# Middle stage of a two-layer spectral convolution kernel: a new order of its product groups, last products in 512 columns, and three of sixteen split units on GpSimd

## The reference, cut to what matters

```python
# layer 0: group norm, upsample by 2, leaky ReLU, downsample by 2
x = x + _filtered_lrelu(_gn(x), f)
# layer 1: spectral convolution of the normalized result
def _contract_tt(xf, a, b, c, d):
    ac, bc, cc, dc = _c(a)[0], _c(b), _c(c), _c(d)[..., 0]
    o1 = jnp.einsum('jxk,ky,bcxy->jbcxy', cc, dc, xf)
    return jnp.einsum('oi,icj,jbcxy->boxy', ac, bc, o1)
x_ft = jnp.fft.rfft2(_gn(x))
out_ft[:, :, :64, :64]  = _contract_tt(x_ft[:, :, :64, :64],  a1, b1, c1, d1)
out_ft[:, :, -64:, :64] = _contract_tt(x_ft[:, :, -64:, :64], a2, b2, c2, d2)
x = x + jnp.fft.irfft2(out_ft, s=(128, 128))
```

## Time and profile before

| | |
|---|---|
| median of 3 runs | 5124.49 us (5120.15 to 5128.3) |
| the profiled execution | 5120.79 us, its span 5118.5 us |
| PE busy | 4679.6 us, 91% of the span |
| DVE busy | 3679.7 us, 72% |
| ACT busy | 3314.3 us, 65% |
| POOL busy | 2581.5 us, 50% |
| first unit to last out group (middle stage) | about 2773 to 4622 us |

### The profile page before, as it was taken

How to read it: one execution, slowest core, us unless ns; L and a number is a source line. 1 busy time by engine, 2 the same in 40 slices (tenths; PEclk the granted TensorE clock), 3 DMA queues, 4 the chain that set the end, 5 groups by cost and what they waited for, 6 DMA issues and landing times. The chain is left out here.

```text
span 5118.5 us, 246321 instructions
## 1 busy us (share of the span) xinstructions
PE 4679.6 (91%) x103206; PEld 4195.3 (82%) x103206; DVE 3679.7 (72%) x5675; ACT 3314.3 (65%) x5910; POOL 2581.5 (50%) x2950
## 2 busy tenths in 40 slices
PE   7999999999999999999984899898989898988999
PEld 6888888888888888888874888888888888888999
DVE  6676777777777777677767888888888888883333
ACT  6767767767677676776854666666666666662332
POOL 7767857768587586776841333333333333330000
PEclk9999999999999999999996999999999999999999
DMA  2131232232321313123232222222222222228999
GB/s 59 57 114 55 63 107 59 65 100 65 106 67 55 114 57 114 57 63 108 65 103 88 82 66 78 70 73 75 68 79 66 82 66 82 66 74 345 420 421 398
DMA packets 609976, 556.29 MB, mean 109 GB/s; under 512 B 16996, under 2 KB 543332, under 8 KB 592612
## 3 DMA queue, kind: packets, MB, share of 16 engines
q1 hardware_dynamic: 609380, 547.21, 32.1%
HBM read 278.71 MB, written 268.44 MB: 107 GB/s over the span
## 5 line engine op out<-in xcount | busy, mean ns | idle before, releaser
L1281 DVE TENSOR_TENSOR Ml<-ring,Mh 128x1024 f16<-128x1024 f32 x1024 | 1199.1, 1217 | 201.6 <-ACT Mh L1248 193.6
L1248 ACT ACTIVATE Mh<-ring 128x1024 f16<-128x1024 f32 x1024 | 986.5, 1022 | 301.5 <-PE ring L1182 301.1
L1182 PE MATMUL ring<-wcur,b_hi 64*128 64x128 f16 x16384 | 749.1, 217 | 176.5 <-DVE Ml L1281 137.2
L752 DVE SCALAR_TENSOR_TENSOR Y<-ring,Y 128x532 f16<-128x532 f32 x1024 | 682.0, 706 | 284.8 <-ACT Y L605 284.6
L267 POOL TENSOR_TENSOR A<-Af,A 128x788 f16<-128x788 f32 x512 | 862.8, 1685 | 41.4
L1182 PEld LDWEIGHTS ring<-wcur,b_hi 64*128 64x128 f16 x16384 | 610.6, 94 | 246.7 <-DVE Ml L1281 154.5
L605 ACT ACTIVATE Y<-ring 128x532 f16<-128x532 f32 x1024 | 575.1, 610 | 275.0 <-PE ring L367 262.2
L1182 PE MATMUL ring<-wcur,b_lo 64*128 64x128 f16 x8192 | 716.9, 217 | 0.0
L367 PE MATMUL ring<-uth,A 64*128 64x138 f16 x12288 | 605.7, 223 | 65.1 <-issue 31.4
L265 POOL CAST A<-Af 128x788 f16<-128x788 f32 x512 | 429.9, 840 | 279.1 <-ACT Af L583 275.2
L767 DVE TENSOR_TENSOR Z<-ring,Z 128x1024 f16<-128x1024 f32 x256 | 313.4, 1224 | 314.7 <-ACT Z L616 314.7
(11 more groups left out here) (153 smaller groups left out, 10436.1 us busy)
## 6 DMA issues: line engine op xcount, KB each, us to landing
xb<-in_x SPq DMA_DIRECT2D x258, 256.0 KB, 2.9
x<-x1b SPq DMA_DIRECT2D x64, 1024.0 KB, 6.4
spec<-sp_out SPq DMA_DIRECT2D x256, 256.0 KB, 3.5
xin<-spec SPq DMA_DIRECT2D x128, 512.0 KB, 6.4
fd<-ft SPq DMA_DIRECT2D x128, 512.0 KB, 4.1
F<-fd SPq DMA_DIRECT2D x64, 1024.0 KB, 20.1
xq<-x SPq DMA_DIRECT2D x64, 1024.0 KB, 16.9
out<-yq SPq DMA_DIRECT2D x64, 1024.0 KB, 18.5
```

The lines of the kernel that those rows point to most:

```text
L752: dve.scalar_tensor_tensor(out=Y[:, e, 1, m], in0=ring[:, pr[u], :, 0:UPS], scalar=0.0, in1=Y[:, e, 0, m], op0=ALU.max, op1=ALU.subtract). ...
L1182: mm = pe.matmul(ring[:, UNIT_PAIR[n], t, 128 * k:128 * k + 128], b[r, z, 4 * u + k, :], wcur[r, z, w, :], start=(part == 0), stop=(part = ...
L1248: act.activation(hi, ps, ACT.Copy).then_inc(e_hi, 1)
L1281: dve.tensor_tensor(lo, ps, hi, ALU.subtract).then_inc(e_lo, 1)
```

## The change

`GROUPS_AT` replaces the three tuples: two groups of app1 after unit 2 and two after unit 5, two out groups of the first spectrum ("out0") after unit 8, two groups of app0 after 11 and two after 13, two out groups of the second spectrum ("out1") after 15. An out group now takes one spectrum and the whole batch: two fp32 matmuls of 512 columns. ScalarE copies out0's result to a new tile `o0`, and VectorE combines `o0` with out1's PSUM result in four operations of 512 columns in place of eight of 256.

Units 1, 5 and 13 (`POOLED`) are no longer split from PSUM: ScalarE copies them in fp32 to a new tile `Mf` (two buffers), which releases the bank pair, and GpSimd makes high and low part from `Mf`. VectorE does nothing for them. GpSimd's list becomes `iteration`: two splits, the row copy of z = 0, the conversion of z = 1, the third split, the row copy of z = 1, the conversion of z = 0 for the next s. SyncE loads before it stores. The shared counters give way to one semaphore for each kind.

```diff
-APP1_AT, OUT_AT, APP0_AT = (3, 3, 5, 5), (7, 7, 9, 9), (11, 11, 14, 14)
+GROUPS_AT = (("app1", (2, 5)), ("out0", (8,)), ("app0", (11, 13)), ("out1", (15,)))
+POOLED = (1, 5, 13)
+DIRECT = tuple(n for n in range(16) if n not in POOLED)
...
+        def released(eng, s, n):
+            if n in POOLED:
+                wait(eng, e_cp, len(POOLED) * s + POOLED.index(n) + 1)
+            else:
+                wait(eng, e_lo, len(DIRECT) * s + DIRECT.index(n) + 1)
...  GpSimd
+            def split(s, i):
+                n = len(POOLED) * s + i + 1
+                _ps, hi, lo = unit(*divmod(POOLED[i], 8))
+                pool.wait_ge(e_cp, n)
+                carry(pool, carried)
+                pool.tensor_copy(hi, Mf[:, i % 2]).then_inc(e_ph, 1)
+                pool.wait_ge(e_ph, n)
+                pool.tensor_tensor(lo, Mf[:, i % 2], hi, ALU.subtract).then_inc(e_pl, 1)
+
+            def iteration(s, more=True):
+                split(s, 0)
+                split(s, 1)
+                if more:
+                    pool.wait_ge(p_bld, 32 * s + 16)
+                    carry(pool, carried)
+                    current(s + 1, 0)
+                convert(s, 1)
+                split(s, 2)
+                if more:
+                    pool.wait_ge(p_bld, 32 * s + 32)
+                    carry(pool, carried)
+                    current(s + 1, 1)
+                    convert(s + 1, 0)
...  TensorE, build
                 if n == 15:
-                    pe.wait_ge(e_lo, 16 * s + 14)
+                    released(pe, s, 13)
                 elif n >= 3:
-                    pe.wait_ge(e_lo, 16 * s + n - 2)
-                elif n == 0 and not isinstance(s, int):
-                    pe.wait_ge(e_lo, 16 * s - 3)
-                elif n == 1:
-                    wait(pe, e_lo, 16 * s)
+                    released(pe, s, n - 3)
+                elif not isinstance(s, int):
+                    released(pe, s - 1, (12, 15, 14)[n])
...  TensorE, apply
                 if j == 0:
-                    pe.wait_ge(e_lo, 16 * s + 8 * z + 8)
+                    pe.wait_ge(e_lo, len(DIRECT) * s + (6, 13)[z])
+                    pe.wait_ge(e_pl, len(POOLED) * s + (2, 3)[z])
                     pe.wait_ge(x_cv[z], s + 1)
...  TensorE, out
+                for r in range(2):
+                    mm = pe.matmul(ring[:, AUX, u, :], am[:, z, r, C * u:C * u + C],
+                                   pout[:, z, r].rearrange("p b y -> p (b y)"), start=(r == 0), stop=(r == 1))
+                mm.then_inc((p_o0, p_o1)[z], 1)
...  ScalarE
+                if n in POOLED:
+                    i = POOLED.index(n)
+                    wait(act, e_pl, len(POOLED) * s + (0, -1, 1)[i])
+                    act.activation(Mf[:, i % 2], ps, ACT.Copy).then_inc(e_cp, 1)
...
+                    act.activation(o0[:, j], ring[:, AUX, j], ACT.Copy).then_inc(e_o0, 1)
```

More of the change, by code:

```diff
@@ L1086, in modes, with unit, groups @@
         e_lo = sem("e_lo")
-        p_aux = sem("p_aux")
-        e_tmp = sem("e_tmp")
-        e_aux = sem("e_aux")
+        e_cp = sem("e_cp")
+        e_ph = sem("e_ph")
+        e_pl = sem("e_pl")
+        p_a = [sem("p_a0"), sem("p_a1")]
+        p_o0, p_o1 = sem("p_o0"), sem("p_o1")
+        e_t = [sem("e_t0"), sem("e_t1")]
+        e_a = [sem("e_a0"), sem("e_a1")]
+        e_o0, e_o1 = sem("e_o0"), sem("e_o1")
         f_st = [sem("f_st0"), sem("f_st1")]
         carried = sem("carried2")
[L1093 to L1101, removed]
+        def released(eng, s, n):
[3 more added lines that the diff above has]
+                wait(eng, e_lo, len(DIRECT) * s + DIRECT.index(n) + 1)
+        def unit(z, u):
+            return (ring[:, UNIT_PAIR[8 * z + u]].rearrange("c k (m y) -> c y k m", y=MODES),
+                    Mh[:, z].rearrange("c y (k m) -> c y k m", k=2)[:, :, :, 8 * u:8 * u + 8],
+                    Ml[:, z].rearrange("c y (k m) -> c y k m", k=2)[:, :, :, 8 * u:8 * u + 8])
+        def groups(n, first, last):
+            for kind, at in GROUPS_AT:
+                if n in at and not (first and kind != "app0") and not (last and kind == "app0"):
+                    for j in range(2):
+                        yield kind, 2 * at.index(n) + j
         block = ctx.enter_context(nc.Block())
@@ L1148, in convert @@
                 pool.wait_ge(x_cv[z], s + 1)
+            def split(s, i):
[20 more added lines that the diff above has]
+                    convert(s + 1, 0)
             for z in range(2):
                 current(0, z)
[L1152 to L1162, removed]
+            convert(0, 0)
+            iteration(0)
+            with pool.Fori(1, MODES - 1) as s:
+                iteration(s)
+            iteration(MODES - 1, more=False)
         @block.tensor
@@ L1198, in apply @@
                                    start=False, stop=True)
[L1199 to L1210, removed]
@@ L1222, in _, with group @@
+            def group(s, kind, j, last=False):
+                if kind == "app0":
+                    apply(s, 0, j)
+                elif kind == "app1":
+                    apply(s - 1, 1, j)
+                elif kind == "out0":
+                    out(s - 1, 0, j, last)
+                else:
+                    out(s - 1, 1, j, last)
             for n in range(16):
                 build(0, n)
-                for i, kind, j in aux_groups(n):
-                    if kind == "app0":
-                        group(0, i, kind, j)
+                for kind, j in groups(n, True, False):
+                    group(0, kind, j)
@@ L1229, in _ @@
                     build(s, n)
-                    for i, kind, j in aux_groups(n):
-                        group(s, i, kind, j)
+                    for kind, j in groups(n, False, False):
+                        group(s, kind, j)
             for n in range(16):
[L1233 to L1241, removed]
+                for kind, j in groups(n, False, True):
+                    group(MODES, kind, j, True)
         @block.scalar
@@ L1312, in iteration @@
                     build(s, n)
-                    for i, kind, j in aux_groups(n):
-                        group(s, i, kind, j, alone, stored)
+                    for kind, j in groups(n, False, False):
+                        group(s, kind, j, alone, stored)
+            dve.sem_inc(e_o1, 2)
             for n in range(16):
                 build(0, n)
-                for i, kind, j in aux_groups(n):
-                    if kind == "app0":
-                        group(0, i, kind, j)
+                for kind, j in groups(n, True, False):
+                    group(0, kind, j)
             iteration(1, alone=True, stored=False)
@@ L1324, in _ @@
             for n in range(16):
-                for i, kind, j in aux_groups(n):
-                    if kind != "app0":
-                        group(MODES, i, kind, j)
+                for kind, j in groups(n, False, True):
+                    group(MODES, kind, j)
 def phase3(nc, fd, x1, iy_d, ix_d, out):
```

112 lines of the change are left out of this document (63 added, 49 removed).

## The result

| | before | changed | ratio, 95% interval |
|---|---|---|---|
| median, us | 5122.3 | 4953.4 (4948.8 to 4961.8, 4 runs) | 0.967 (0.965 to 0.969) |
| the profiled execution, us (span) | 5120.8 (5118.5) | 4952.5 (4950.7) | |
| one iteration of the loop, us | 28.68 | 25.97 | |
| first unit to the last stage's first matmul, us | 1862.1 | 1698.7 | |

What follows compares the result with a forecast made beforehand. TensorE, held up by waits for VectorE, was taken as nearest to the bound. 63 iterations saving 2.57 us (162), less 7, gave 155 off 5120.8: 4966 profiled, 4968 us median forecast; range 4930 to 5020.

Steps and rivals of the forecast that it cites:

- What bounds the kernel, and TensorE's own pace: In the loop, TensorE is nearest to full and waits for VectorE; without waits its iteration takes 25.4 of 28.68 us.
- The loop's end: Unit 1 waits for unit 15's banks; two out groups between them remove about 2.4 us an iteration.
- The wait that is left: Before the third app0 group, a walk through one iteration leaves TensorE waiting 0.7 us for VectorE's sum; period 26.1 us.
- Units 5 and 7: Their banks are released 0.1 us before TensorE asks; they could add a few tenths of a us.
- The choice of the first stage's rows over the row of the same size: GpSimd's split priced by contiguous first-stage splits at 3.3 us, with 4.8 from the same-size conversions as upper end.
- rival C: GpSimd's writes of Mh in short pieces cost extra; at 6.5 us a split, 5310 us; chance 0.04 including interference with VectorE.
- The joins: Seven gaps between operations in GpSimd's list, at 0.1 to 0.57 us each, 1.5 us in its 21.8 us sum.
- The crossing point: GpSimd's list exceeds the old 28.7 us iteration, making the change slower, when a split exceeds 5.6 us.
- rival B: GpSimd becomes the loop's bound, its list 26.3 or 27.6 us, giving 4983 or 5065 us; chance 0.12 (4998 to 5100).
- rival D: GpSimd's work slows VectorE's subtractions beyond 1.23 us; price here nil, chance 0.02.
- The 512 columns: Out groups in half as many TensorE instructions gain 0 to 0.2 us an iteration, taken as 0.05.
- Start and end: First app0 group 6.6 us later behind two splits, second iteration 2.5 more, 2 back at the end: net loss 7 us.

Runs made afterwards that it cites:

- the kernel in which no matmul is recorded waiting: Changed kernel with the first two app0 groups after unit 10 instead of 11: 4920.7 us, 0.961 of the kernel before, period 25.38 us.
- the kernel with three casts: Changed kernel with three further GpSimd casts to an unread tile ahead of each split: 5234.8 us, 1.024 of the kernel before, period 30.37 us.
- the kernel with two casts: Changed kernel with two further GpSimd casts to an unread tile ahead of each split: 5021.6 us, period 26.92 us.

## Why the prediction was right

**What bounds the kernel, and TensorE's own pace.** Right. 25.4 us was worked out twice; the kernel in which no matmul is recorded waiting runs at 25.38.

**The loop's end.** Right, and shown by itself: put in place of the two out groups' cover, the wait of 1.6 us returns. The prediction priced it at 2.4 us of the 3.2 lost; moving out1 by one unit costs 1.91. The other 0.5 was unit 15's own wait, which does not return there, since ScalarE's copy of unit 13 still releases its banks. Before, unit 1 came 0.76 + 2.49 us after unit 15, less two units of 0.67 the same 1.91.

**The wait that is left.** Right in place, a little large in size. The walk put VectorE's ninth unit at 1.96, the first app0 sum at 5.38 and the third group at 5.82 us behind out0. VectorE's timeline has, out0 ending at about 3517.5:

```profile
3519.55 3.49 DVE L1328 TENSOR_TENSOR Ml<-ring,Mh 128x1024 f16<-128x1024 f32 x3 [2.26 <-ACT Mh L1291]
3522.95 0.75 DVE L1337 TENSOR_TENSOR pout<-ring,tmp 128x256 f32<-128x256 f32 x2
```

and TensorE:

```profile
3523.42 0.19 PE L1237 MATMUL ring<-xs,Mh 128*128 128x32 f16 x1 [0.52 <-DVE pout L1337]
```

The wait costs 25.97 - 25.38 = 0.59 us of period, not 0.7: the walk set it beside TensorE's last unit without the ordinary turn of 0.1 us, which is in the 25.4 already. Units 5 and 7, which it feared for a few tenths, do not wait. So the period came out at 25.97, not 26.1.

**GpSimd.** The choice of the first stage's rows over the row of the same size was right to a hundredth. One step to it was luck. The ten-element pieces of the earlier trace rows lie on the side that is read (`Af`), the eight-element pieces of `Mh` on the side that is written, so those rows did not bear on rival C. A run does: in the kernel with three casts the contiguous cast to `spare` takes 1039 ns and the one to `Mh` from the same tile 1041. (The 3.27 us of the prediction are 3.25 by its own terms.)

The joins were too dear. Beside its waits for ScalarE the list occupies 25.97 - 5.9 = 20.1 us, not 21.8. Operations that wait for nothing start before the one ahead has ended by the record, and behind a conversion there is a gap of about 0.5 us, once an iteration where the list is the bound. There, with splits of 5.17 and 6.14 us, the list is 26.5 and 29.45 us, in both 11.0 beside the three splits. The prediction's sum has 12.0 (row copies 1.0, conversions 9.5, joins 1.5), and gives 27.5 and 30.4 against periods of 26.92 and 30.37. That the second agrees is luck: 1 us too much for joins stands where the wait for unit 13's copy is.

The crossing point, put at a split of 5.6 us, lies between 5.17 and 6.14, around 5.7 on the line between them. So rivals B and C had the mechanism right: a list that is long enough becomes the bound. Their price was not right. Even with splits as dear as conversions the list would be 11.0 + 14.3 = 25.3 us by estimate, below the period, so rival B's 26.3 and 27.6 stood on joins that were too dear.

The GPSIMD Engine Reference of the Trainium skill, in its section on performance pitfalls for Q7 kernels, has a factor of 1.5 for reads with more than 8 bytes between elements, and the prediction's estimate from it was 3.1 us for a split; the two operations took 1.04 + 2.13. The direction agrees; the two factors measured are 1.89 for the cast and 1.28 for the subtraction.

**VectorE and ScalarE.** Four 512-column operations take 0.68 us by record and start 0.60 apart, against 0.63 by thirds. The subtraction's mean is 1219 ns, from 1217: rival D's interference is nothing that shows (1216 with no unit on GpSimd).

**The 512 columns.** 0.04 us an iteration against 0.05.

**Start and end.** The first app0 group starts 21.4 us after the first unit, 16.7 before: 4.7 later, not 6.6. From the first unit to the last stage's first matmul 163.4 us are saved; 63 x 2.71 = 170.9, so start and end lose 7.5 against the 7 of the sum. The total agrees though its first term was 2 us too large; the second iteration and the end, 2.5 and -2 in the sum, were not measured apart.

**The sum.** 155 us were forecast from the execution of before, 168 came: 8 from the period (63 x 0.14 = 9, less 0.5) and 4.4 because the first unit starts at 2768.5 and not at 2772.9 us. The code ahead of it is the same, and over the kernels run here GpSimd's first row copy of the middle stage stands anywhere from 2763.0 to 2785.9 us, so that can't be put down to the change.

## What to carry to other kernels

Where several engines work through a ring of buffers in an order fixed by hand, look at each reuse of a buffer and count what its last user's list holds between filling and release, and what the first engine's list holds meanwhile; engine totals do not tell it. Here one number that put long matmuls between two users of one bank pair was worth 120 us, 1.9 us of each iteration, while taking 3.4 us of work per iteration off an engine was worth 0.7 to 0.85. When the distribution of work changes, walk the places again, since the best one moves with it. And price an operation that an engine has not done yet by rows of its own access form, not of its size.

## What the runs showed of the hardware that was not expected

TensorE's granted clock fell to the lower level once an iteration where it stood still for 3.6 us (0.51 in the 7 us from the middle of the wait on), while waits of 1.6 us, one in each iteration before, left the stretch from 3100 to 4247.2 us at 1.00. The length of the wait alone does not tell it: in the kernel with two casts the longest wait was 1.3 us, and behind one such wait the clock fell (0.94 over that iteration, 0.98 from 3100 to 4144 us). On GpSimd, 1024 elements from fp32 to fp16 took 1.04 us read contiguously and 1.96 us read with a step of 512 bytes; the subtraction behind it 2.13 and 2.72.
